# A recurrent layer in which tanh of g and i becomes one instruction and the scan reads two row halves

## The reference, cut to what matters

```python
xi = xt @ U_i + b_i; xf = ...; xg = xt @ U_c + b_c; xo = xt @ U_o + b_o
def step(carry, xs):
    h, c = carry
    i_t = jax.nn.sigmoid(xi_t + h @ V_i)
    f_t = jax.nn.sigmoid(xf_t + h @ V_f)
    g_t = jnp.tanh(xg_t + h @ V_c)
    o_t = jax.nn.sigmoid(xo_t + h @ V_o)
    c_new = h * c + i_t * g_t
    h_new = o_t * jnp.tanh(c_new)
    return ((h_new, c_new), h_new)
```

## Time and profile before

| | us |
|---|---|
| median of 3 runs | 826.31 (824.18 to 826.82) |
| span of the profiled execution | 836.2 |
| recurrent steps within it (499.2 to 831.7) | 332.5 |
| PE busy / DVE busy / ACT busy, whole span | 734.4 / 339.7 / 288.9 |
| mean granted TensorE clock, whole span | 0.807 |

### The profile page before, as it was taken

How to read it: one execution, slowest core, us unless ns; L and a number is a source line. 1 busy time by engine, 2 the same in 40 slices (tenths; PEclk the granted TensorE clock), 3 DMA queues, 4 the chain that set the end, 5 groups by cost and what they waited for, 6 DMA issues and landing times.

```text
span 836.2 us, 13956 instructions
## 1 busy us (share of the span) xinstructions
PE 734.4 (88%) x5217; PEld 396.0 (47%) x5224; DVE 339.7 (41%) x1247; ACT 288.9 (35%) x1390; POOL 126.4 (15%) x146
## 2 busy tenths in 40 slices
PE   6899999999999999998998978888888888888886
PEld 3555555656665655544333843333433333343333
DVE  4444434444434344434546053333333333333333
ACT  2322222222222222212531014444444444444443
POOL 3333333333333333410000000000000000000000
PEclk9666655565556566667999989999899999999999
DMA  7000000000000000000000000000000000000000
GB/s 259 1 1 2 2 0 0 0 0 0 0 0 0 0 0 0 0 0 1 0 1 0 1 1 1 1 1 2 1 1 1 2 1 2 2 2 1 2 1 14
DMA packets 2578, 6.30 MB, mean 8 GB/s; under 512 B 1372, under 2 KB 1953, under 8 KB 2337
## 3 DMA queue, kind: packets, MB, share of 16 engines
q1 hardware_dynamic: 2530, 5.68, 2.0%
HBM read 5.42 MB, written 0.26 MB: 7 GB/s over the span
## 4 chain that ended last, share of the span: by engine, by line
PE 60%; DVE 19%; ACT 15%; issue 6%; POOL 1%; another core or an unknown queue 0%; DVEq 0%; POOLq 0%
PE bk L311 15%; PE bk L638 10%; DVE bk L1077 6%; ACT gp L803 5%; DVE mem L1080 5%; ACT bk L804 5%; ACT bk L808 4%; PE bk L524 4%; PE bk L423 4%; PE bk L595 3%; DVE a0y L907 2%; PE bk L433 2%; PE bk L375 1%; PE bk L542 1%; DVE hv L905 1%
## 5 line engine op out<-in xcount | busy, mean ns | idle before, releaser
L654 PE MATMUL bk<-idle 128*64 128x512 bf16 x720 | 203.0, 388 | 0.0
L638 PEld LDWEIGHTS bk<-mem,lvh 65*64 65x64 f32 x1536 | 82.0, 139 | 181.8 <-DVE mem L1080 181.6
L638 PE MATMUL bk<-mem,lvh 65*64 65x4 f32 x1536 | 104.5, 208 | 59.3 <-DVE mem L1080 59.3
L311 PE MATMUL bk<-idle 128*128 128x256 bf16 x608 | 146.5, 395 | 2.2 <-POOL lrcur L258 2.2
L1077 DVE TENSOR_TENSOR_SCAN bk<-bk,gp 64x12 f32<-64x12 f32 x256 | 46.4, 181 | 146.9 <-ACT bk L804 146.9
L803 ACT ACTIVATE gp<-bk 64x8 f32<-64x8 f32 x256 | 43.8, 171 | 151.7 <-PE bk L638 151.7
L311 PEld LDWEIGHTS bk<-idle 128*128 128x128 bf16 x608 | 67.1, 129 | 42.3 <-issue 11.5
L654 PEld LDWEIGHTS bk<-idle 128*64 128x64 bf16 x720 | 61.7, 113 | 23.3 <-issue 2.0
L274 POOL TENSOR_TENSOR mem<-mem,gcur 128x1024 f32<-128x1024 f32 x16 | 30.3, 1893 | 213.1 <-DVE mem L934 212.9
L1080 DVE SCALAR_TENSOR_TENSOR mem<-og,bk 64x4 f32<-64x4 f32 x256 | 38.3, 150 | 53.7 <-ACT bk L808 53.7
L806 ACT ACTIVATE og<-bk 64x4 f32<-64x4 f32 x256 | 42.8, 167 | 6.1
(11 more groups left out here) (273 smaller groups left out, 850.3 us busy)
## 6 DMA issues: line engine op xcount, KB each, us to landing
cw<-in_cw SPq DMA_DIRECT2D x1, 3456.0 KB, 10.9
w<-in_w SPq DMA_DIRECT2D x1, 520.0 KB
w<-in_w SPq DMA_DIRECT2D x1, 512.0 KB
xs<-in_x SPq DMA_DIRECT2D x1, 256.0 KB, 2.6
out<-xs SPq DMA_DIRECT2D x1, 256.0 KB, 2.1
memw<-in_memw SPq DMA_DIRECT2D x1, 128.0 KB, 2.1
wqkv<-in_wqkv SPq DMA_DIRECT2D x1, 96.0 KB, 2.3
c1p<-in_c1p SPq DMA_DIRECT2D x1, 66.0 KB
```

What stands on the lines that cost most here:

```text
L311: nc.tensor.matmul(bk[:, bank, 0:256], idle[:, 0:128], idle[:, 128:128 + 256], start=True, stop=True)
L638: return nc.tensor.matmul(bk[row:row + D, 2 * (s // CH % 2) + k, c:c + B], lvh[:, g, :], hist[:, s, :], start=False, stop=True, skip_group ...
L654: nc.tensor.matmul(bk[0:D, 5, 0:FILL_N], idle[:, 0:D], idle[:, 128:128 + FILL_N], start=True, stop=True)
```

## The change

- **Gates.** g (rows 0 to 63) and i (rows 64 to 127) lie at the same columns of one bank; one tanh reads all 128 rows and writes `gx[:, :, 2]`, a new SBUF tile of 128 x 4 x 4. Since i needs tanh(i/2), its weights are halved beforehand (`lvh` by another half, `luh` as a scaled copy of `lu`, six small DVE instructions in an earlier stage).
- **Scan.** (add, multiply) over 4 x 4 elements, in0 from the upper rows of `gx`, in1 from the lower. Per sequence: (.. + 0) * 0 clears, (0 + 1) * 1 = 1, (1 + tanh(i/2)) * g, (that + h*c) * 1. The h * c instruction writes rows 64 to 127 of `gx`.
- **Input products.** Chunks of 16, 112 and 128 steps in place of sixteen of 16. The second is made in steps 2 to 9, the third in steps 20 to 48 at every fourth, in quarters: 112 or 128 columns each; g and i together in four steps, o alone in four.
- **Fillers.** Two of 512 columns in a step, one in the sixteen steps with input products, over 128 output columns in place of 64.

```diff
-CH = 16
-FILL, FILL_N = 3, 512
+CHUNKS = (0, 16, 128, S)
+FILL, FILL_N = 2, 512
...
+def chunk_of(s):
+    return 0 if s < CHUNKS[1] else 1 if s < CHUNKS[2] else 2
+def columns(s):
+    c = (s - CHUNKS[chunk_of(s)]) * B
+    return slice(c, c + B)
...
-        gp = sb("gp", [D, B, 3])
+        luh = sb("luh", [D + 1, 3, D])
+        gx = sb("gx", [128, B, 4])
-        cs = bk[0:D, 4, 0:6 * B].rearrange("p (n b k) -> p n b k", n=2, b=B)
+        cs = bk[0:D, 4, 0:8 * B].rearrange("p (n b k) -> p n b k", n=2, b=B)
...
-            def inputs_part(chunk, g):
+            def inputs_part(chunk, g, part, parts):
                 k, row = gate_at[g]
-                nc.tensor.matmul(bk[row:row + D, 2 * (chunk % 2) + k, 0:CH * B], lu[:, g, :], t3T[:, chunk * CH:(chunk + 1) * CH, :],
-                                 start=True, stop=False, skip_group_check=True)
+                n = (CHUNKS[chunk + 1] - CHUNKS[chunk]) // parts
+                nc.tensor.matmul(bk[row:row + D, 2 * (chunk % 2) + k, part * n * B:(part + 1) * n * B], luh[:, g, :],
+                                 t3T[:, CHUNKS[chunk] + part * n:CHUNKS[chunk] + (part + 1) * n, :], start=(part == 0), stop=False,
+                                 skip_group_check=True)
...
+            ahead = {2 + k: (1, k % 4) for k in range(8)}
+            ahead.update({20 + 4 * k: (2, k % 4) for k in range(8)})
...
                 fills = FILL
-                if 2 <= s % CH < 5 and s // CH + 1 < S // CH:
-                    inputs_part(s // CH + 1, s % CH - 2)
-                    fills = max(fills - 1, 0)
+                if s in ahead:
+                    chunk, part = ahead[s]
+                    fills = FILL - 1
+                    if s < 6 or 20 <= s < 36:
+                        inputs_part(chunk, 0, part, 4)
+                        inputs_part(chunk, 1, part, 4)
+                    else:
+                        inputs_part(chunk, 2, part, 4)
                 for _ in range(fills if s + 1 < S else 0):
-                    nc.tensor.matmul(bk[0:D, 5, 0:FILL_N], idle[:, 0:D], idle[:, 128:128 + FILL_N], start=True, stop=True)
+                    nc.tensor.matmul(bk[:, 5, 0:FILL_N], idle[:, 0:128], idle[:, 128:128 + FILL_N], start=True, stop=True)
...
-                nc.scalar.activation(gp[:, :, 0:2], wide(bk[0:D, bank, cols], 2), ACT.Tanh)
-                nc.scalar.activation(bk[0:D, 6, 1:3 * B:3], bk[D:2 * D, bank, cols], ACT.Tanh, scale=0.5).then_inc(sem("in_gate"), 1)
+                nc.scalar.activation(gx[:, :, 2], bk[:, bank, cols], ACT.Tanh).then_inc(sem("in_gate"), 1)
...
-            nc.vector.tensor_scalar(lvh[0:D, :, :], lv[:, :, :], 0.5, None, ALU.mult)
+            for g, part_of in enumerate((1.0, 0.5, 1.0)):
+                nc.vector.tensor_scalar(lvh[0:D, g, :], lv[:, g, :], 0.5 * part_of, None, ALU.mult)
+                nc.vector.tensor_scalar(luh[:, g, :], lu[:, g, :], part_of, None, ALU.mult)
+            nc.vector.memset(gx[0:D, :, 3], 1.0)
+            nc.vector.memset(gx[:, :, 1], 1.0).then_inc(sem("rec_set"), 1)
...
-            link(nc.vector.memset(bk[0:D, 6, 0:32], 0.0))
-            nc.vector.memset(bk[0:D, 6, 2:3 * B:3], 1.0).then_inc(sem("rec_init"), 1)
...
-                nc.vector.tensor_tensor_scan(c_t.rearrange(flat3), bk[0:D, 6, 0:3 * B], gp[:, :, :].rearrange(flat3),
-                                             0.0, ALU.mult, ALU.add).then_inc(sem("c_new"), 1)
+                nc.vector.tensor_tensor_scan(c_t.rearrange(flat4), gx[D:2 * D, :, :].rearrange(flat4), gx[0:D, :, :].rearrange(flat4),
+                                             0.0, ALU.add, ALU.mult).then_inc(sem("c_new"), 1)
...
-                    nc.vector.scalar_tensor_tensor(gp[:, :, 2], hist[0:D, s + 1, :], 0.5, c_t[:, :, 2], ALU.mult,
+                    nc.vector.scalar_tensor_tensor(gx[D:2 * D, :, 3], hist[0:D, s + 1, :], 0.5, c_t[:, :, 3], ALU.mult,
```

More of the change, by code:

```diff
@@ L246, in _ @@
             nc.gpsimd.memset(sc0[:, :, :], 0.0)
-            nc.gpsimd.memset(gp[:, :, :], 0.0)
+            nc.gpsimd.memset(gx[:, :, :], 0.0)
             for t in (*img, *zim):
@@ L623, in _ @@
                     ins.then_inc(sem("t3T_ps"), 1)
-            pe.wait_ge(sem("ld_l"), 32)
+            pe.wait_ge(sem("rec_set"), 1)
             pe.wait_ge(sem("t3T"), 3)
             gate_at = ((0, 0), (0, D), (1, 0))
-            def inputs_part(chunk, g):
+            def inputs_part(chunk, g, part, parts):
                 k, row = gate_at[g]
-                nc.tensor.matmul(bk[row:row + D, 2 * (chunk % 2) + k, 0:CH * B], lu[:, g, :], t3T[:, chunk * CH:(chunk + 1) * CH, :],
-                                 start=True, stop=False, skip_group_check=True)
+                n = (CHUNKS[chunk + 1] - CHUNKS[chunk]) // parts
+                nc.tensor.matmul(bk[row:row + D, 2 * (chunk % 2) + k, part * n * B:(part + 1) * n * B], luh[:, g, :],
+                                 t3T[:, CHUNKS[chunk] + part * n:CHUNKS[chunk] + (part + 1) * n, :], start=(part == 0), stop=False,
+                                 skip_group_check=True)
             def recurrent(s, g):
                 k, row = gate_at[g]
-                c = s % CH * B
-                return nc.tensor.matmul(bk[row:row + D, 2 * (s // CH % 2) + k, c:c + B], lvh[:, g, :], hist[:, s, :],
+                return nc.tensor.matmul(bk[row:row + D, 2 * (chunk_of(s) % 2) + k, columns(s)], lvh[:, g, :], hist[:, s, :],
                                         start=False, stop=True, skip_group_check=True)
+            ahead = {2 + k: (1, k % 4) for k in range(8)}
+            ahead.update({20 + 4 * k: (2, k % 4) for k in range(8)})
             for g in range(3):
-                inputs_part(0, g)
+                inputs_part(0, g, 0, 1)
             pe.wait_ge(sem("h_zeros"), 1)
@@ L797, in _ @@
             table(ACT.Tanh)
-            act.wait_ge(sem("rec_init"), 1)
+            act.wait_ge(sem("rec_set"), 1)
             for s in range(S):
-                cols = slice(s % CH * B, (s % CH + 1) * B)
-                bank = 2 * (s // CH % 2)
+                cols = columns(s)
+                bank = 2 * (chunk_of(s) % 2)
                 act.wait_ge(sem("gates_ig"), s + 1)
-                nc.scalar.activation(gp[:, :, 0:2], wide(bk[0:D, bank, cols], 2), ACT.Tanh)
-                nc.scalar.activation(bk[0:D, 6, 1:3 * B:3], bk[D:2 * D, bank, cols], ACT.Tanh, scale=0.5).then_inc(sem("in_gate"), 1)
+                nc.scalar.activation(gx[:, :, 2], bk[:, bank, cols], ACT.Tanh).then_inc(sem("in_gate"), 1)
                 act.wait_ge(sem("gate_o"), s + 1)
@@ L807, in _ @@
                 act.wait_ge(sem("c_new"), s + 1)
-                nc.scalar.activation(bk[0:D, 6, 16:16 + B], cs[:, s % 2, :, 2], ACT.Tanh, scale=0.5).then_inc(sem("tanh_c"), 1)
+                nc.scalar.activation(bk[0:D, 6, 16:16 + B], cs[:, s % 2, :, 3], ACT.Tanh, scale=0.5).then_inc(sem("tanh_c"), 1)
         @block.vector
@@ L1067, in _ @@
                 ins.then_inc(sem("t3T"), 1)
-            link(nc.vector.memset(bk[0:D, 6, 0:32], 0.0))
-            nc.vector.memset(bk[0:D, 6, 2:3 * B:3], 1.0).then_inc(sem("rec_init"), 1)
             nc.vector.memset(og[:, :], 0.0).then_inc(sem("h_new"), 1)
-            flat3 = "p b k -> p (b k)"
+            flat4 = "p b k -> p (b k)"
             for s in range(S):
```

## The result

The changed kernel took **875.25 us** (median of 4 runs, 868.78 to 881.17) against 826.57 us of the kernel before (4 runs beside it, 824.18 to 833.97): ratio 1.0545, 95% interval 1.0463 to 1.0627, so slower. I had forecast 785.8 with a range of 783 to 812. The profiled execution took 877.69 us with a span of 875.9.

The account below looks back on a forecast made before the run. The loop's ring of waits without slack was taken as the bound, mostly at 2.4 GHz (chance 0.57). Ring -39.7, low-clock stretches -0.7, memsets -0.1: 836.2 - 40.5 = 795.7 us profiled, 785.8 as median; range 783 to 812.

Parts of the forecast that it names:

- The ring: Loop's slackless chain of waits PE, tanh, scan, tanh of c, h: a step falls from 1.29 to 1.14 us, saving 39.7.
- the o gate: Its tanh, run behind the new activation, stays hidden before tanh of c, by 0.06 us a step.
- The scan's fixed time: Scan on DVE: 156 to 158 ns fixed whether an input is in PSUM or SBUF; whole scan 181 to 190 ns.
- Large chunks and preparation: Bigger input products cost nothing; extra DVE scalings and memsets before the loop hide in a 2.6 us wait, else 1 us.
- PE: fillers and input products: PE in the loop at 2.4 GHz: both cost nothing, hidden by about 0.28 us idle a step waiting for h.
- a clock that goes up and down: Rival in the loop: half of the steps at the low clock, 12 us more, 798 us; chance 0.22.
- thirteen of fifteen groups passed: Old loop's groups of steps with two fillers and an input product: thirteen passed without a clock fall; evidence against the up-and-down clock.
- With two fillers: 1.66 - 0.43 = 1.23 us: Loop step at 1.2 GHz: the old PE-bound 1.66 us less one filler's turn of 0.43.
- the prediction's own ring at this clock: Loop's chain at 1.2 GHz: 0.81 us outside PE and 0.43 on PE.
- rival 4: Loop at 1.2 GHz: 128-column fillers leave no free columns, products wait 0.18 us; 1.41 a step, 854 us; chance 0.03.
- a clock low throughout: Rival in the loop: clock stays at 1.2 GHz from the start, 808.6 us, up to 821; chance 0.12.

Follow-up runs that it names:

- `lead`: Changed kernel with three fillers of 64 columns in its first 10 loop steps, then two of 128 as changed: 872.62 us, ratio 1.0506.
- `hold`: Changed kernel with three fillers of 64 columns in its first 64 loop steps (two in those with input products), then two of 128 as changed: 847.01 us.

## Why the prediction was wrong

**The ring: right.** I had 0.155 us a step from one tanh and the scan. The version with the fillers of before measured 294.1 / 256 = 1.149 a step against the predicted 1.135, 786.67 us against 785.8. The tanh over both halves took 178 ns, not 167, and that is most of the difference; the scan 192 against 190; the o gate stayed hidden.

**The scan's fixed time: right.** It is 192 - 16 x 2.08 = 159 ns with both inputs in SBUF. The rule of the Trainium skill (VectorE: DVE Perf Modes, on the TRN2 errata) would have made it 65 ns shorter; nothing of that shows.

**Large chunks and preparation: right.** The loop with chunks of 16 and that with three large ones are both 294.10 us. The wait that was to hide the preparation is still there, 2.3 us where it was 2.6; this row of the groups by line answers to it:

```profile
L1032 DVE CAST QV<-W8T 8x512 bf16<-8x512 f32 x2 | 0.8, 411 | 2.3 <-ACT W8T L796 2.3
```

**"PE: fillers and input products ... costed at nothing": the first step that failed.** It was argued "while the clock is at 2.4 GHz", and the step that gave this clock its chance (0.57, and 0.22 for a clock that goes up and down) was the wrong one. The loop stood at 0.50 from start to end. I had seen that three fillers held and that both falls came where two stood, and called it undecided; then I let the falls' rarity (thirteen of fifteen groups passed) decide. Those groups were three steps each, with three fillers in the steps around them; in the new loop there is no third filler to lift the clock again. The kernel before with the two fillers alone, on 64 or on 128 columns, stood at 0.50 in all its loop. The rule that I weighed, of the Trainium skill (TensorE: Matmul & The Clock Gate, Why this matters for your kernels), warns of long idle gaps; PE's records fill 6.00 of the 6.00 us from 600 to 606 after the change, and the clock stayed down. That a loop without gaps holds the clock isn't borne out.

**"With two fillers: 1.66 - 0.43 = 1.23 us": the second step that failed.** It takes away a filler of 64 columns and forecasts a step with fillers of 128. For 64 columns the step was 1.25, but set by the ring, as the run without fillers shows; the prediction's own ring at this clock, 0.81 + 0.43 = 1.24, was right. For 128 it is 1.487, 0.24 more, because products and fillers now wait for one another. I had this case as rival 4, at 1.41 a step and 854 us, with a chance of 0.03. It fell short by 0.08 a step. Some 0.06 of it is its price, 0.18 from the filler's tail where 0.24 was measured, of which 0.11 lies ahead of the products and 0.13, which it didn't count, between them and the fillers. The rest is the 1.23 that it started from. Its reason, that the filler leaves no free columns, was wrong: 32 columns do the same. Its chance was wrong most of all: of the 0.12 for a clock low throughout, nothing in the rows said that fillers of another shape would behave like those in the trace. The Trainium skill has the rule (TensorEngine Tiling (Array Packing), Key Properties): changing the tiling mode, not just the tile, drains TensorE. I hadn't drawn on it. The waits ahead of the weight load, for four pairs of widths, agree with it; if they are this drain, its price here is 0.24 us a step at 1.2 GHz.

Both together: 256 x (1.487 - 1.14) = 89 us between forecast and result in the loop. 256 x (1.25 - 1.14) = 28 of them are the low clock by itself, 256 x 0.24 = 61 the shapes. Against the kernel before, the gain of 38 us is covered and 48 us of loss are laid on it. A slip without weight: the chances that the range leaves out add up to 0.06 + 0.04 + 0.03 + 0.02 = 0.15, not to about 0.17.

**What stays open.** Why the clock rises in one loop and not in another isn't settled. Two fillers of 64 columns raised it in the new ring (1.25 a step) and never in the old one (1.39), with the same recurrent products and fillers on PE. Two of 128, at 1.49 or 1.52, never did in the four kernels that have them from early on (the change, `lead`, and the two above with the old ring and with wide products), nor did two of 32 or none at all, and three of 128 did after 44 and 54 us. Three of 64 did within some 3 us in three profiles and in ten steps of `lead` not at all. The number that tells them apart wasn't found. Nor is it known how far the width by itself, rather than the longer step that it makes, keeps the clock down. The 38 us that two fillers of 128 held it were seen once. That PE drains in the 0.30 us is the reading of a rule and four pairs; no record shows it, and the wide products, whose load doesn't wait, gained no time by it.

## What to carry to other kernels

Give a filler the output width of the work that it stands beside, by changing the filler and not the work. Where the width differed here, it cost nothing while PE had slack and became the bound when the clock was low. Price a change of the fillers by itself and at the lower clock first: a step that only the high clock hides has the price of the low one with the whole chance that the clock falls. And when a latency saving and a cut of the fillers come in one change, measure the saving with the old fillers; here that version is 4.9% faster than the kernel before and the combined one 5.5% slower.

## What the runs showed of the hardware that I had not expected

- The weights of a product whose output width differs from that of the matmul ahead of it are loaded late: 0.29 to 0.30 us behind h at 1.2 GHz for 64 behind 128 and for 64 behind 32, 0.05 for equal widths. At 2.4 GHz, with three fillers of 128 in a step of 1.15 us, the load comes 0.05 behind h, but the fillers' load comes 0.32 us behind the products' in place of 0.23.
- Two fp32 products of 128 columns are slower than three of 64: at 2.4 GHz with three fillers in both 0.42 us from the first load to the tanh against 0.34, and 1.24 us a step against 1.15. At 1.2 GHz it is 0.64 against 0.43, of which 0.17 pass before the first product starts.
- The clock can stay low without idle gaps on PE: 234 us after the fall in `hold` with PE recorded as busy in all of them, and 380.7 us after the change with 367.8 busy.
